# Running the second normalisation inside the last expert, with the short tile moved to the first unit

## The chip, the cores and the metric

One core of a Trainium2 chip runs the whole kernel. The metric is the device time in microseconds (us), median of three runs. Times in the text are us unless marked ns.

## The reference, cut to what matters

```
x = x + attention(x);  x = layernorm(x)            # (8, 1024, 256), no scale or bias
scores = softmax(x @ router_w.T)                   # 8 experts
gate, idx = top_k(scores per batch and expert, 257 tokens)
y = gelu(x[idx] @ w1 + b1) @ w2 + b2               # hidden width 1024
x = layernorm(x + scatter_add(y * gate at idx))    # the second normalisation
```

Each expert takes 257 tokens of each of the 8 batches. `layernorm` subtracts the mean of a row of 256 and divides by the square root of variance plus 1e-5.

## The kernel before, in words

The program is a row of stages: latent, attention, output projection with the first normalisation, the choice of tokens, the experts (`expert_stage`), and the second normalisation (`final_stage`). A stage is a block of its own: all engines meet at its end, and the next stage begins after that. Rows of `x` after the first normalisation stand in `x1_d` in HBM, with a second copy in `acc_d`, into which the experts add.

**Tiles and units (L1136 to L1141).** 257 tokens are two full tiles of 128 and one token left over. The left-over tokens of the 8 batches form one short tile of 8 rows. So an expert has 17 tiles: (batch 0, 0), (batch 0, 1), (batch 1, 0) and so on, and the short one last. `STARTS` cuts them into five units of 4, 4, 3, 3 and 3 tiles, with 512, 512, 384, 384 and 264 tokens.

**A unit on the engines.** GpSimd (POOL) gathers the token rows by an indirect DMA for each tile (L1258), two units ahead. TensorE (PE) transposes them (L1312), ScalarE (ACT) and VectorE (DVE) split them into a high and a low part. PE makes eight chunks of the hidden layer, each of six products (L1328 to L1330). ACT applies gelu (L1392), DVE splits the result (L1435, L1430). PE transposes the next unit's tokens, then makes the outputs of each tile with 24 products (L1343 to L1345). DVE adds the bias into `yb` (L1453), ACT multiplies by the gate into `yg` (L1381), and POOL adds the rows into `acc_d` by one indirect DMA a tile (`scatter`, L1262 to L1274), once the whole unit's `yg` is there. Buffers: four `raw` between gelu and split, four PSUM banks for hidden chunks, four output slots in PSUM, two each of `tok` and `yg`. Each engine runs its own list in program order. On ACT a unit is: eight gelus, split of the next tokens, gating (`gated`). On DVE: eight splits, low part of the next tokens, the bias adds. On POOL (`unit`, L1281): gather for two units ahead, a quarter of the next expert's weights (L1279, not in the last expert), scatter. So the eighth expert's ACT and DVE lists go on to the next unit only when the current unit's `yb` and `yg` are done.

**The end of the expert stage.** POOL waits for the landing of all scatters (L1294), SyncE (SP) has only loads of weights and biases to issue.

**The final stage (L1461 to L1549).** `acc_d` is cut into 16 groups of 512 rows, two to a batch, each held as 128 partitions of 4 rows. SP loads a group (four buffers). DVE measures it: four `bn_stats`, four `bn_aggr` (L1523, L1527). POOL turns the variance into the reciprocal root by two small instructions (L1504, L1506). DVE subtracts and scales in four passes (L1536) into a second buffer, and ACT's queue stores it to `out` (L1513).

Of the kernel before, what the change touches and what calls it, by code (L numbers as in the profile page):

```python
# [16 lines left out]
P = 128  # L17
# [1107 lines left out]
            sp.wait_ge(left_in, 32)  # L1125


def expert_stage(nc, w1, b1, w2, b2, W, x1_d, acc_d, idx_all, gate_all, idx_left, gate_left):

# [1 line left out]

    TILES = [(b, f, P) for b in range(B) for f in range(FULL)] + [(None, None, B)]  # L1136
    STARTS = [0, 4, 8, 11, 14, len(TILES)]
    UNITS = len(STARTS) - 1
    HC = HID // P
    YT = len(TILES)  # L1140
    HB = 4  # L1141
    RB = 4
    with ExitStack() as ctx:
        sb = lambda n, s, d=F32: ctx.enter_context(nc.sbuf_tensor(n, s, d))
        pb = lambda n, s, d=F32: ctx.enter_context(nc.psum_tensor(n, s, d))
# [13 lines left out]
        hid_lo = sb("hid_lo", [P, HC, HALF], F32R)  # L1159
        yb = sb("yb", [P, 4, C])  # L1160
        yg = [sb(f"yg{i}", [P, 4, C]) for i in range(2)]
        t_ps = [pb(f"e_t{i}", [P, HALF]) for i in range(2)]
        h_ps = [pb(f"e_h{i}", [P, HALF]) for i in range(HB)]
        y_ps = [pb(f"e_y{i}", [P, 2, C]) for i in range(2)]
# [1 line left out]
        b_in = [sem(f"b_in{u}") for u in range(2)]  # L1166
        tok_in = [sem(f"tok_in{i}") for i in range(2)]
        put = [sem(f"put{i}") for i in range(UNITS)]
        lists, turned, t_high, t_low, h_done, gelu_done, h_high, h_low, y_done, b_done, g_done = (
            sem(n) for n in ("lists", "turned", "t_high", "t_low", "h_done", "gelu_done", "h_high", "h_low",  # L1170
                             "y_done", "b_done", "g_done"))
# [5 lines left out]
        def tiles(g):  # L1177

            return [(q, *t) for q, t in enumerate(TILES[STARTS[g]:STARTS[g + 1]])]

        def batches(g):

            return {c for _, b, _, _ in tiles(g) for c in (range(B) if b is None else (b,))}

        def later(n, u, g, by, last):

# [9 lines left out]
        def landed(eng, g, n):  # L1196

            if not (isinstance(n, int) and n == 0):
                eng.wait_ge(put[g], 16 * len(tiles(g)) * n)
# [15 lines left out]
        def _(sp):  # L1215
# [19 lines left out]
            with sp.Fori(0, NE // 2 - 1) as i:  # L1235
                for u in range(2):
                    expert(2 * i + u, u)

        @block.gpsimd
        def _(pool):  # L1240
# [5 lines left out]
            pool.wait_ge(const_ready, 1)  # L1246
            pool.affine_select(out=ident[:], in_=ident[:], compare_op=ALU.not_equal, fill=1.0, base=0,
                               pattern=[[-1, P]], channel_multiplier=1).then_inc(const_ready, 1)

            def rows_of(u, b, f):  # L1250
                return idl[u][:, 0:1] if b is None else idx[u][:, f, b:b + 1]
# [29 lines left out]
            def unit(n, u, g, last):  # L1281

                ahead = later(n, u, g, 2, last)
                if ahead:
                    pool.wait_ge(turned, 2 * UNITS * n + 2 * g + 2)
                    gather(*ahead)
                if g < 4 and not (last and u == 1):
                    weights_low(n + 1, 1 - u, g)
                scatter(n, u, g)

            gather(0, 0, 0)
            gather(0, 0, 1)
            over_experts(pool, unit)
            for g in range(UNITS):  # L1294
                landed(pool, g, NE)

        @block.tensor
        def _(pe):
# [109 lines left out]
        def _(dve):  # L1408
# [15 lines left out]
            def unit(n, u, g, last):  # L1424
# [19 lines left out]
                if g == 2 and not (last and u == 1):  # L1444

                    for o in range(UNITS):
                        landed(dve, o, n)
                    make_lists(n + 1, 1 - u)
                for q, _, _, rows in tiles(g):
                    dve.wait_ge(y_done, YT * n + STARTS[g] + min(q // 2 * 2 + 2, len(tiles(g))))  # L1450

                    dve.wait_ge(g_done, YT * n + STARTS[g] + 1)
                    dve.tensor_tensor(yb[0:rows, q, :], y_ps[q // 2][0:rows, q % 2, :], b2s[u][0:rows, :],  # L1453
                                      ALU.add).then_inc(b_done, 1)

            make_lists(0, 0)
            tokens_low(0, 0, 0)
            over_experts(dve, unit)


def final_stage(nc, acc_d, out):  # L1461

    G = NTOK // HALF
    BUFS = 4
    with ExitStack() as ctx:  # L1465
        sb = lambda n, s, d=F32: ctx.enter_context(nc.sbuf_tensor(n, s, d))
        sem = lambda n: ctx.enter_context(nc.semaphore(n))
        expo = sb("f_expo", [P, 4])
        a = [sb(f"f_a{v}", [P, 4, C]) for v in range(BUFS)]
        o = [sb(f"f_o{v}", [P, 4, C]) for v in range(BUFS)]  # L1470
        stats = [sb(f"f_stats{v}", [P, 4, 6]) for v in range(2)]
        mv = [sb(f"f_mv{v}", [P, 4, 2]) for v in range(2)]
        rstd = [sb(f"f_rstd{v}", [P, 4]) for v in range(2)]
        a_in = [sem(f"f_a_in{v}") for v in range(BUFS)]
        o_out = [sem(f"f_o_out{v}") for v in range(BUFS)]
        passed = sem("f_passed")
        const_ready, stat_done, mv_done, var_done, rstd_done, o_done = (
            sem("f_" + n) for n in ("const", "stat_done", "mv_done", "var_done", "rstd_done", "o_done"))
        block = ctx.enter_context(nc.Block())
        rows = lambda d, i: d.rearrange("(g j p) c -> g p j c", p=P, j=4)[bass.ds(i, 1), :, :, :].rearrange(  # L1480
            "o p j c -> p (o j) c")

        @block.sync
        def _(sp):
            for v in range(BUFS):
                sp.dma_start(a[v][:], rows(acc_d, v)).then_inc(a_in[v], 16)
            with sp.Fori(1, G // BUFS) as i:
                for v in range(BUFS):

                    sp.wait_ge(o_done, BUFS * i + v - BUFS + 1)  # L1490
                    sp.dma_start(a[v][:], rows(acc_d, BUFS * i + v)).then_inc(a_in[v], 16)

        @block.gpsimd
        def _(pool):
            for v in range(BUFS):
                pool.sem_inc(o_out[v], 1)
            pool.memset(expo[:], -0.5).then_inc(const_ready, 1)
            pool.wait_ge(const_ready, 1)
            with pool.Fori(0, G // 2) as i:  # L1499
                for v in range(2):  # L1500
                    n = 2 * i + v
                    pool.wait_ge(mv_done, n + 1)
                    pool.sem_inc(passed, 1)  # L1503
                    pool.tensor_scalar(rstd[v][:], mv[v][:, :, 1], EPS, 1.0, ALU.add, ALU.mult).then_inc(var_done, 1)  # L1504
                    pool.wait_ge(var_done, n + 1)
                    pool.tensor_tensor(rstd[v][:], rstd[v][:], expo[:], ALU.pow).then_inc(rstd_done, 1)  # L1506

        @block.scalar
        def _(act):
            with act.Fori(0, G // BUFS) as i:  # L1510
                for v in range(BUFS):
                    act.wait_ge(o_done, BUFS * i + v + 1)
                    act.dma_start(rows(out, BUFS * i + v), o[v][:]).then_inc(o_out[v], 16)  # L1513
            for v in range(BUFS):
                act.wait_ge(o_out[v], 16 * (G // BUFS) + 1)

        @block.vector
        def _(dve):
            def measure(i, v):
                n = BUFS * i + v  # L1520
                dve.wait_ge(a_in[v], 16 * i + 16)
                for j in range(4):
                    dve.bn_stats(stats[v % 2][:, j, :], a[v][:, j, :]).then_inc(stat_done, 1)  # L1523
                for j in range(4):
                    dve.wait_ge(stat_done, 4 * n + j + 1)  # L1525
                    dve.sem_inc(passed, 1)  # L1526
                    ins = dve.bn_aggr(mv[v % 2][:, j, :], stats[v % 2][:, j, :])  # L1527
                ins.then_inc(mv_done, 1)

            def normalise(i, v):  # L1530
                n = BUFS * i + v
                dve.wait_ge(mv_done, n + 1)
                dve.wait_ge(rstd_done, n + 1)
                dve.wait_ge(o_out[v], 16 * i + 1)
                for j in range(4):
                    ins = dve.tensor_scalar(o[v][:, j, :], a[v][:, j, :], mv[v % 2][:, j, 0:1],  # L1536
                                            rstd[v % 2][:, j:j + 1], ALU.subtract, ALU.mult)
                ins.then_inc(o_done, 1)


            measure(0, 0)
            with dve.Fori(0, G // BUFS - 1) as i:  # L1542
                for v in range(BUFS):
                    measure(*((i, v + 1) if v < BUFS - 1 else (i + 1, 0)))
                    normalise(i, v)
            for v in range(BUFS):
                if v < BUFS - 1:
                    measure(G // BUFS - 1, v + 1)
                normalise(G // BUFS - 1, v)  # L1549


def post_ln_attention_moe(nc, x, x_t, w_down, w_k, w_v, w_q, w_out, router_t, w1, b1, w2, b2, out):
# [4 lines left out]
    with ExitStack() as ctx:  # L1557
# [9 lines left out]
        output_stage(nc, x, w_out, router_t, y_d, x1_d, acc_d, prob_all)  # L1567
        W = ExpertWeights(sb, sem)
        choose_stage(nc, w1, w2, W, prob_all, idx_all, gate_all, idx_left, gate_left)
        expert_stage(nc, w1, b1, w2, b2, W, x1_d, acc_d, idx_all, gate_all, idx_left, gate_left)  # L1570
        final_stage(nc, acc_d, out)


# [32 lines left out]
```

## Time and profile before

| | us |
|---|---|
| median of three runs | 3475.12 (3470.42 to 3476.35) |
| the profiled execution's own time | 3469.43 |
| its span, first to last instruction | 3467.5 |
| PE busy in the span | 3185.9 (92%) |
| DVE / ACT / POOL busy | 2097.3 / 1840.7 / 1388.5 |
| PE stage of the last expert | 3299.70 to about 3396.1 |
| first load of the final stage | 3411.20 |

Times in the rows below count from the span's start. Busy time is that of instructions; issue of DMAs on the SP and ACT queues doesn't count. PE's instructions overlap, so the distance between two starts says more than a duration.

### The profile page before, as it was taken

The page shows a single profiled execution, that of the slowest core. Times are in us where ns is not written, and L with a number is a line of the kernel's source. Part 1 is how long each engine was busy: PE and PEld are TensorE (multiplying, and loading weights), DVE is VectorE, ACT ScalarE, POOL GpSimd, SP SyncE. Part 2 cuts the span into 40 slices and gives each one's busy share as a digit, 9 for nine tenths or more (in the row PEclk, how much of TensorE's full clock was granted, in tenths as well). Part 3 has the DMA queues.
Part 4 walks back from the last instruction along what each step waited for, and adds up shares of the span by engine and source line. Part 5 has one row for each costly group of instructions (what it writes and reads, how often), then busy time and mean ns, then how long its engine had stood idle before and what let it go on. Part 6 is the DMA issues. An engine that isn't in the chain of part 4 may idle for free. (4 is left out here: it accounts for less than half of the span.)

```text
span 3467.5 us, 69523 instructions
## 1 busy us (share of the span) xinstructions
PE 3185.9 (92%) x21406; PEld 2506.0 (72%) x21406; DVE 2097.3 (60%) x4881; ACT 1840.7 (53%) x4007; POOL 1388.5 (40%) x1512
## 2 busy tenths in 40 slices
PE   5999999999999999999999999979908999999991
PEld 3767676667667676767676776679908999999991
DVE  1666566666666666666666666657584555455546
ACT  2667566666666666666666666633203343343430
POOL 0434343333334343334333333312214656565543
PEclk7999999999999999999999999989959999999996
DMA  6444444444445444444444444267402333333226
GB/s 204 106 114 108 99 113 104 102 102 119 104 100 123 101 107 110 108 98 114 107 99 117 106 111 101 65 250 268 180 27 64 72 68 74 67 76 68 41 42 202
DMA packets 184386, 376.26 MB, mean 109 GB/s; under 512 B 23872, under 2 KB 108224, under 8 KB 181952
## 3 DMA queue, kind: packets, MB, share of 16 engines
q1 hardware_dynamic: 144704, 308.52, 34.6%
q0 software_dynamic: 29696, 50.48, 7.3%
q10 hardware_dynamic: 9600, 12.58, 1.0%
q8 instruction: 184, 3.01, 0.4%
q14 instruction: 202, 1.65, 0.1%
HBM read 123.97 MB, written 79.76 MB: 59 GB/s over the span
## 5 line engine op out<-in xcount | busy, mean ns | idle before, releaser
L243 POOL TENSOR_SCALAR prob<-prob,inv 128x128 f32<-128x128 f32 (+7 forms) x1024 | 774.9, 757 | 1311.5 <-DVE inv L589 1311.5
L584 DVE TENSOR_REDUCE neg_max<-s_ps 128x1 f32<-128x128 f32 (+7 forms) x1024 | 773.2, 755 | 725.6 <-PE s_ps L370 709.9
L495 ACT ACTIVATE prob<-s_ps,neg_max 128x128 f32<-128x128 f32 (+7 forms) x1024 | 758.0, 741 | 199.6 <-DVE neg_max L584 182.4
L380 PE MATMUL t_ps<-ident,prob 128*128 128x128 f32 x4608 | 683.5, 275 | 9.1 <-ACT prob_t L573 2.5
L368 PE MATMUL s_ps<-k_hh,q_hl 128*128 128x512 f32 (+3 forms) x1536 | 591.6, 385 | 44.6 <-ACT prob L495 26.6
L573 ACT ACTIVATE prob_t<-t_ps 128x512 f32<-128x512 f32 (+3 forms) x768 | 415.8, 541 | 396.9 <-PE t_ps L380 396.2
L396 PE MATMUL o_ps<-prob_t,v 128*64 128x512 f32 (+3 forms) x3072 | 537.5, 492 | 1.5 <-DVE y L606 1.5
L369 PE MATMUL s_ps<-k_lz,q_hl 128*128 128x512 f32 (+3 forms) x1536 | 513.2, 346 | 0.0
L380 PEld LDWEIGHTS t_ps<-ident,prob 128*128 128x128 f32 x4608 | 495.7, 141 | 19.6 <-ACT prob_t L573 14.1
L368 PEld LDWEIGHTS s_ps<-k_hh,q_hl 128*128 128x128 f32 x1536 | 290.9, 189 | 176.4 <-issue 92.0
L396 PEld LDWEIGHTS o_ps<-prob_t,v 128*64 128x64 f32 x3072 | 203.8, 136 | 278.0 <-issue 251.6
L648 DVE COPY prob_t<-t_ps 128x128 f32<-128x128 f32 (+3 forms) x768 | 366.9, 478 | 57.1 <-PE t_ps L380 54.1
L369 PEld LDWEIGHTS s_ps<-k_lz,q_hl 128*128 128x128 f32 x1536 | 292.1, 190 | 32.1
L1343 PE MATMUL e_y<-w_hi,hid_hi 128*128 128x256 f32 (+1 forms) x1088 | 307.2, 282 | 0.0
L1345 PE MATMUL e_y<-w_hi,hid_lo 128*128 128x256 f32 (+1 forms) x1088 | 303.9, 279 | 0.0
L1344 PE MATMUL e_y<-w_lo,hid_hi 128*128 128x256 f32 (+1 forms) x1088 | 303.7, 279 | 0.0
L1271 POOL DMA_INDIRECT acc_d<-yg,idx x128 | 230.9, 1804 | 86.0 <-ACT yg L1381 52.4
L1392 ACT ACTIVATE raw<-e_h,b1s 128x512 f32<-128x512 f32 (+2 forms) x320 | 187.9, 602 | 138.4 <-PE e_h L1330 106.9
L1435 DVE CAST hid_hi<-raw 128x512 fp32r<-128x512 f32 (+2 forms) x320 | 172.6, 546 | 121.7 <-ACT raw L1392 120.8
L370 PE MATMUL s_ps<-mask_b,ident_b 128*128 128x128 bf16 x1024 | 236.2, 231 | 0.0
L1328 PE MATMUL e_h<-tok_hi,w_hi 128*128 128x384 f32 (+2 forms) x640 | 225.6, 352 | 4.4 <-issue 4.4
L1381 ACT ACTIVATE yg<-yb,gate 128x256 f32<-128x256 f32 x128 | 59.3, 503 | 320.2 <-DVE yb L1453 320.2
(152 smaller groups left out, 5502.7 us busy)
## 6 DMA issues: line engine op xcount, KB each, us to landing
k_hh<-k_high SPq DMA_DIRECT2D x256, 256.0 KB, 4.6
q_hl<-q_high SPq DMA_DIRECT2D x128, 256.0 KB, 4.0
q_hl<-q_low SPq DMA_DIRECT2D x128, 256.0 KB, 4.2
k_lz<-k_low SPq DMA_DIRECT2D x128, 256.0 KB, 5.4
y_d<-y SPq DMA_DIRECT2D x128, 256.0 KB, 3.8
c_yt<-y_d SPq DMA_DIRECT2D x16, 2048.0 KB, 8.5
w_raw<-w SPq DMA_DIRECT2D x16, 1024.0 KB, 7.5
a_xt<-x_t SPq DMA_DIRECT2D x8, 1024.0 KB, 7.6
```

What stands on the lines that cost most here:

```text
L243: pool.tensor_scalar(pr, pr, inv[:, s % 4:s % 4 + 1], 1.0, ALU.mult, ALU.mult).then_inc(norm_done, 1)
L368: pe.matmul(out, q_hl[u][h][:, cols], k_hh[u][h][:, w], start=True, stop=False)
L369: pe.matmul(out, q_hl[u][h][:, cols], k_lz[u][h][:, w], start=False, stop=True)
L380: mm = pe.transpose(t_ps[k % 2][:, j * P:(j + 1) * P], prob[s % 4][:, (first + j) * P:(first + j + 1) * P], ident[:])
L396: mm = pe.matmul(o_ps[64 * h:64 * h + 64, off:HALF], v[u][:, k, 64 * h:64 * h + 64], prob_t[g][:, h, k, off:HALF], start=(k == 0), stop=(k ...
L495: act.activation(prob[s % 4][:, 0:(q + 1) * P], s_ps[s % 2][:, 0:(q + 1) * P], ACT.Exp, bias=neg_max[:, s % 4:s % 4 + 1], accum_out=total[ ...
L573: act.activation(prob_t[g][:, h, b0:b0 + count, q % 4 * P:(q % 4 + 1) * P], t_ps[0][:, 0:count * P].rearrange("p (j c) -> p j c", c=P), AC ...
L584: dve.tensor_reduce(neg_max[:, s % 4:s % 4 + 1], s_ps[s % 2][:, 0:(q + 1) * P], AX.X, ALU.max, negate=True).then_inc(max_done, 1)
L648: dve.tensor_copy(prob_t[g][:, h, b0:b0 + count, q % 4 * P:(q % 4 + 1) * P], t_ps[1][:, 0:count * P].rearrange("p (j c) -> p j c", c=P)).t ...
L1343: pe.matmul(out, hid_hi[:, m, cols], W.w2_hi[u][:, w], start=(m == 0), stop=False)
L1344: pe.matmul(out, hid_hi[:, m, cols], W.w2_lo[u][:, w], start=False, stop=False)
L1345: mm = pe.matmul(out, hid_lo[:, m, cols], W.w2_hi[u][:, w], start=False, stop=(m == HC - 1))
```

## The change

`final_stage` is gone, and its work is in `expert_stage`. The short tile stands at place 3, and `STARTS` gives units of 4, 4, 4, 3 and 2 tiles (392, 512, 512, 384 and 256 tokens), in all eight experts. A batch ends with the unit that holds its second full tile: `ended(0)` is groups 0 and 1, `ended(1)` 2 to 5, `ended(2)` 6 to 9, `ended(3)` 10 to 13, `ended(4)` 14 and 15. In the last expert:

- SP waits for each unit's scatters to land and loads the groups that it ended into six buffers `fin`; group i needs the store of group i-6 landed.
- DVE measures the groups of the unit before: two ahead of its first bias add, two ahead of its third (in the unit of two tiles: behind its bias adds).
- POOL, after a unit's scatter, does for each group of the unit before the reciprocal root (`spread`) and, for groups 0 to 11, the four passes in place and the store from its own queue (`close`).
- DVE closes groups 12 to 15 behind everything, and SP stores them.

```
-    TILES = [(b, f, P) for b in range(B) for f in range(FULL)] + [(None, None, B)]
-    STARTS = [0, 4, 8, 11, 14, len(TILES)]
+    TILES = [(b, f, P) for b in range(B) for f in range(FULL)]
+    TILES.insert(3, (None, None, B))
+    STARTS = [0, 4, 8, 12, 15, len(TILES)]
+    G = NTOK // HALF;  FB = 6;  BY_POOL = G - 4
# SP, behind its loop over experts
+            for g in range(UNITS):
+                landed(sp, g, NE)
+                for i in ended(g):
+                    if i >= FB:
+                        sp.wait_ge(f_out[i % FB], 16 * (i // FB))
+                    sp.dma_start(fin[i % FB][:], rows_out(acc_d, i)).then_inc(f_in[i % FB], 16)
+            for i in range(BY_POOL, G):
+                sp.wait_ge(f_closed, i - BY_POOL + 1)
+                sp.dma_start(rows_out(out, i), fin[i % FB][:]).then_inc(f_last, 16)
# POOL
+            def spread(i):
+                pool.wait_ge(f_mv, i + 1)
+                pool.tensor_scalar(rstd[v][:], mv[v][:, :, 1], EPS, 1.0, ALU.add, ALU.mult).then_inc(f_var, 1)
+                pool.wait_ge(f_var, i + 1)
+                pool.tensor_tensor(rstd[v][:], rstd[v][:], expo[:], ALU.pow).then_inc(f_rstd, 1)
+            def close(i):
+                pool.wait_ge(f_rstd, i + 1)
+                for j in range(4):
+                    pool.tensor_scalar(fin[v][:, j, :], fin[v][:, j, :], mv[v][:, j, 0:1], rstd[v][:, j:j + 1],
+                                       ALU.subtract, ALU.mult).then_inc(f_scaled, 1)
+                pool.wait_ge(f_scaled, 4 * i + 4)
+                pool.dma_start(rows_out(out, i), fin[v][:]).then_inc(f_out[v], 16)
# POOL, unit()
                 scatter(n, u, g)
+                if last and u == 1 and g:
+                    for i in ended(g - 1):
+                        spread(i)
+                        if i < BY_POOL:
+                            close(i)
# DVE, unit()
+                closing = ended(g - 1) if last and u == 1 and g else []
+                for i in closing[:2]:
+                    measure(i)
                 for q, _, _, rows in tiles(g):
+                    if q == 2:
+                        for i in closing[2:]:
+                            measure(i)
                     (bias add of tile q)
+                if len(tiles(g)) <= 2:
+                    for i in closing[2:]:
+                        measure(i)
# at the end: POOL spread(14), spread(15); DVE close(12), close(13), measure(14), measure(15), close(14), close(15)
```

## Rows read from the trace of the kernel before

**Rows 1.** Windows: span; PE, PEld, DVE, ACT, POOL busy (count); granted clock; DMA.
```profile
3299.70:3396.20 96.50, 96.42 (x676) 90.52 (x674) 45.78 (x106) 35.05 (x65) 40.40 (x28) 1.00 0.25 38
...
3411.20:3467.50 56.30, 0.00 (x0) 0.00 (x0) 48.32 (x192) 0.00 (x0) 20.93 (x33) 0.50 0.89 298
```

**Rows 2.** Timeline of PE, last expert: start, duration, engine, line, operation.
```profile
3299.70 0.39 PE L1328 MATMUL e_h<-tok_hi,w_hi 128*128 128x512 f32 x1
...
3310.89 1.04 PE L1312 MATMUL e_t<-e_ident,tok 128*128 128x128 f32 x8
3311.68 0.36 PE L1343 MATMUL e_y<-w_hi,hid_hi 128*128 128x256 f32 x1
...
3323.08 0.40 PE L1328 MATMUL e_h<-tok_hi,w_hi 128*128 128x512 f32 x1
...
3372.14 1.05 PE L1312 MATMUL e_t<-e_ident,tok 128*128 128x128 f32 x6
3373.13 0.39 PE L1343 MATMUL e_y<-w_hi,hid_hi 128*128 128x256 f32 x1
```

**Rows 3.** Timeline of DVE and POOL, last expert: bias add, scatters.
```profile
3323.28 0.76 DVE L1453 TENSOR_TENSOR yb<-e_y,b2s 128x256 f32<-128x256 f32 x2 [4.84 <-PE e_y L1345]
...
3325.59 1.72 POOL L1271 DMA_INDIRECT acc_d<-yg,idx  x1 [13.24 <-ACT yg L1381]
...
3331.41 2.03 POOL L1271 DMA_INDIRECT acc_d<-yg,idx  x1 [0.30 <-issue]
...
3401.70 1.35 POOL L1271 DMA_INDIRECT acc_d<-yg,idl  x1 [0.30 <-issue]
```

**Rows 4.** Timeline of the final stage, its beginning and its last passes.
```profile
3411.20 2.22 SPq L1486 DMA_DIRECT2D f_a<-acc_d  x4
...
3415.07 1.41 DVE L1523 BATCH_NORM_STATS2 f_stats<-f_a 128x6 f32<-128x256 f32 x4 [18.49 <-DMA f_a<-acc_d]
3416.39 0.41 DVE L1527 BATCH_NORM_AGGREGATE f_mv<-f_stats 128x2 f32<-128x6 f32 x4
...
3418.60 1.38 DVE L1536 TENSOR_SCALAR f_o<-f_a,f_mv,f_rstd 128x256 f32<-128x256 f32 x4
3418.77 0.30 POOL L1504 TENSOR_SCALAR f_rstd<-f_mv 128x4 f32<-128x4 f32 x1 [0.43 <-DVE f_mv L1527]
3419.15 1.05 POOL L1506 TENSOR_TENSOR f_rstd<-f_rstd,f_expo 128x4 f32<-128x4 f32 x1
...
3462.54 1.39 DVE L1536 TENSOR_SCALAR f_o<-f_a,f_mv,f_rstd 128x256 f32<-128x256 f32 x4 [0.32 <-issue]
```

**Rows 5.** Groups by form, POOL: count | busy us, mean ns of one | idle.
```profile
L243 POOL TENSOR_SCALAR prob<-prob,inv 128x256 f32<-128x256 f32 x128 | 63.4, 496 | 189.2 <-DVE inv L589 189.2
...
L772 POOL DMA_DIRECT2D x_d<-c_x x16 | 12.9, 809 | 35.7 <-DVE c_x L897 35.7
```

**Rows 6.** DMA issues: queue, count, KB each, median us from issue to landing.
```profile
x_d<-c_x POOLq DMA_DIRECT2D x16, 512.0 KB, 4.5
...
f_a<-acc_d SPq DMA_DIRECT2D x16, 512.0 KB, 5.2
...
acc_d<-yg,idx POOLq DMA_INDIRECT x128, 3.9
```

**Rows 7.** Timeline of POOL and DVE, around the end of the seventh expert.
```profile
3286.84 2.40 POOL L1279 TENSOR_TENSOR w_lo<-w_raw,w_hi 128x1024 fp32r<-128x1024 f32 x1 [2.20 <-ACT w_hi L1365]
...
3291.39 3.64 POOL L1271 DMA_INDIRECT acc_d<-yg,idx  x1 [0.30 <-issue]
...
3301.24 1.01 POOL L1258 DMA_INDIRECT tok<-x_d,idx  x1 [0.30 <-issue]
```

**Rows 8.** Timeline of DVE in the same stretch.
```profile
3287.16 2.44 DVE L1435 CAST hid_hi<-raw 128x264 fp32r<-128x264 f32 x2 [1.89 <-ACT raw L1392]
...
3290.41 0.29 DVE L1435 CAST hid_hi<-raw 128x264 fp32r<-128x264 f32 x1
...
3290.96 0.28 DVE L1435 CAST hid_hi<-raw 128x264 fp32r<-128x264 f32 x1
```

More of the change, by code:

```diff
@@ L1125, in _, with expert_stage @@
             sp.wait_ge(left_in, 32)
-def expert_stage(nc, w1, b1, w2, b2, W, x1_d, acc_d, idx_all, gate_all, idx_left, gate_left):
-    TILES = [(b, f, P) for b in range(B) for f in range(FULL)] + [(None, None, B)]
-    STARTS = [0, 4, 8, 11, 14, len(TILES)]
+def expert_stage(nc, w1, b1, w2, b2, W, x1_d, acc_d, idx_all, gate_all, idx_left, gate_left, out):
+    TILES = [(b, f, P) for b in range(B) for f in range(FULL)]
+    TILES.insert(3, (None, None, B))
+    STARTS = [0, 4, 8, 12, 15, len(TILES)]
     UNITS = len(STARTS) - 1
@@ L1142, in expert_stage @@
     RB = 4
+    G = NTOK // HALF
+    FB = 6
+    BY_POOL = G - 4
     with ExitStack() as ctx:
@@ L1161, in expert_stage @@
         yg = [sb(f"yg{i}", [P, 4, C]) for i in range(2)]
+        expo = sb("f_expo", [P, 4])
+        fin = [sb(f"f_a{v}", [P, 4, C]) for v in range(FB)]
+        stats = [sb(f"f_stats{v}", [P, 4, 6]) for v in range(FB)]
+        mv = [sb(f"f_mv{v}", [P, 4, 2]) for v in range(FB)]
+        rstd = [sb(f"f_rstd{v}", [P, 4]) for v in range(FB)]
         t_ps = [pb(f"e_t{i}", [P, HALF]) for i in range(2)]
@@ L1168, in expert_stage @@
         put = [sem(f"put{i}") for i in range(UNITS)]
+        f_in = [sem(f"f_in{v}") for v in range(FB)]
+        f_out = [sem(f"f_out{v}") for v in range(FB)]
+        f_stat, f_mv, f_var, f_rstd, f_scaled, f_closed, f_last = (
+            sem(n) for n in ("f_stat", "f_mv", "f_var", "f_rstd", "f_scaled", "f_closed", "f_last"))
         lists, turned, t_high, t_low, h_done, gelu_done, h_high, h_low, y_done, b_done, g_done = (
@@ L1183, in batches, with ended @@
             return {c for _, b, _, _ in tiles(g) for c in (range(B) if b is None else (b,))}
+        def ended(g):
+            ends = {max(i for i, t in enumerate(TILES) if t[0] == b): b for b in range(B)}
+            return [2 * ends[i] + h for i in range(STARTS[g], STARTS[g + 1]) if i in ends for h in range(2)]
+        rows_out = lambda d, i: d.rearrange("(g j p) c -> g p j c", p=P, j=4)[i]
         def later(n, u, g, by, last):
@@ L1237, in _ @@
                     expert(2 * i + u, u)
+            for g in range(UNITS):
[7 more added lines that the diff above has]
+                sp.dma_start(rows_out(out, i), fin[i % FB][:]).then_inc(f_last, 16)
+            for v in range(FB):
+                sp.wait_ge(f_out[v], 16 * len(range(v, BY_POOL, FB)))
+            sp.wait_ge(f_last, 16 * (G - BY_POOL))
         @block.gpsimd
@@ L1248, in _ @@
                                pattern=[[-1, P]], channel_multiplier=1).then_inc(const_ready, 1)
+            pool.memset(expo[:], -0.5).then_inc(const_ready, 1)
+            pool.wait_ge(const_ready, 3)
+            def spread(i):
+                v = i % FB
+                pool.wait_ge(f_mv, i + 1)
+                pool.sem_inc(passed, 1)
+                pool.tensor_scalar(rstd[v][:], mv[v][:, :, 1], EPS, 1.0, ALU.add, ALU.mult).then_inc(f_var, 1)
+                pool.wait_ge(f_var, i + 1)
+                pool.tensor_tensor(rstd[v][:], rstd[v][:], expo[:], ALU.pow).then_inc(f_rstd, 1)
+            def close(i):
+                v = i % FB
+                pool.wait_ge(f_rstd, i + 1)
+                pool.sem_inc(passed, 1)
+                for j in range(4):
[3 more added lines that the diff above has]
+                pool.dma_start(rows_out(out, i), fin[v][:]).then_inc(f_out[v], 16)
             def rows_of(u, b, f):
@@ L1293, in _ @@
             over_experts(pool, unit)
-            for g in range(UNITS):
-                landed(pool, g, NE)
+            for i in ended(UNITS - 1):
+                spread(i)
         @block.tensor
@@ L1454, in unit, with measure, close @@
                                       ALU.add).then_inc(b_done, 1)
+                if len(tiles(g)) <= 2:
+                    for i in closing[2:]:
+                        measure(i)
+            def measure(i):
+                v = i % FB
+                dve.wait_ge(f_in[v], 16 * (i // FB) + 16)
+                for j in range(4):
+                    dve.bn_stats(stats[v][:, j, :], fin[v][:, j, :]).then_inc(f_stat, 1)
+                for j in range(4):
+                    dve.wait_ge(f_stat, 4 * i + j + 1)
+                    dve.sem_inc(passed, 1)
+                    ins = dve.bn_aggr(mv[v][:, j, :], stats[v][:, j, :])
+                ins.then_inc(f_mv, 1)
+            def close(i):
+                v = i % FB
+                dve.wait_ge(f_rstd, i + 1)
+                for j in range(4):
+                    ins = dve.tensor_scalar(fin[v][:, j, :], fin[v][:, j, :], mv[v][:, j, 0:1], rstd[v][:, j:j + 1],
+                                            ALU.subtract, ALU.mult)
+                ins.then_inc(f_closed, 1)
             make_lists(0, 0)
@@ L1458, in _ @@
             over_experts(dve, unit)
[L1461 to L1549, printed above, removed]
@@ L1552, in post_ln_attention_moe @@
+            for i in range(BY_POOL, ended(UNITS - 1)[0]):
+                close(i)
+            for i in ended(UNITS - 1):
+                measure(i)
+            for i in ended(UNITS - 1):
+                close(i)
 def post_ln_attention_moe(nc, x, x_t, w_down, w_k, w_v, w_q, w_out, router_t, w1, b1, w2, b2, out):
@@ L1569, in post_ln_attention_moe @@
         choose_stage(nc, w1, w2, W, prob_all, idx_all, gate_all, idx_left, gate_left)
-        expert_stage(nc, w1, b1, w2, b2, W, x1_d, acc_d, idx_all, gate_all, idx_left, gate_left)
-        final_stage(nc, acc_d, out)
+        expert_stage(nc, w1, b1, w2, b2, W, x1_d, acc_d, idx_all, gate_all, idx_left, gate_left, out)
 def kernel(**inputs):
```

## The prediction

> **What bounds the kernel now.** I read the windows first. In the last expert PE is busy for 96.42 of 96.50 us at full granted clock, POOL for 40.40 and DVE for 45.78 [rows 1]: PE sets the time, and DVE and POOL have room. In the final stage PE does nothing and DVE is busy for 48.32 of 56.30 us [rows 1]: DVE sets the time there, and POOL has 35 us free. Between them lies a hand-over: the last scatter is issued until 3403.05 [rows 3] and the first load starts at 3411.20 [rows 4]. From PE's end (3396.1) to the span's end (3467.5) are 71.4 us in which PE is idle. The change can only win there. The profiled execution's time is 3469.43, 1.9 over its span, and 5.7 under the median of the runs; I work out the difference in its span and put it on the median.
>
> **Units, all experts.** PE's starts give 11.19 for a hidden part of 512 tokens, 0.79 for the eight transposes behind it, 11.40 for the outputs of four tiles (2.85 a tile); where the short tile is among the transposed ones, 0.99 [rows 2]. By width, 392, 384 and 256 tokens take 8.57, 8.39 and 5.6. The widths sum to 2056 before and after and there are 17 tiles, so PE's work is the same; fewer transposes fall beside the slow short ones, which I estimate at -0.2 an expert. For seven experts that is -1, so the last one starts at 3298.7 instead of 3299.7. Times below count from there.
>
> Two gathers get closer to their use. POOL's fourth gather of the next expert's unit 1 starts at 3301.24 [rows 7]. No row shows a gather's landing; the scatter's 3.9 [rows 6] bounds it from above, and nothing excludes 1.0, its issue. By the bound it lands at 3305.1. Before, PE wants it at 3310.89 [rows 2]; now the last unit is 2.8 shorter and the first one's hidden part 2.6, so it wants it at 3305.5. The gather of unit 0 gains a tile of scatter (1.96) ahead of it and comes as close. Both fit, by 0.4 at worst. I cost them at nothing; if that cover goes, each us late costs 14 us (two places, seven experts).
>
> **The last expert, PE.** Units end at 20.8, 44.1, 67.3, 84.7 and, if nothing waits, 96.0.
>
> **Prices.** A scatter of four tiles takes 7.85 (3325.59 to 3333.44), so 1.96 a tile, and starts 1.55 behind the end of the last bias add [rows 3]. A scatter lands 3.9 after its issue, a POOL store 4.5 [rows 6]. A load takes 3.9 alone [rows 4] and 5.2 in the crowd [rows 6]; I take 3.9 for the first, 1.75 more for each next one of a burst (0.5 MB at 298 GB/s [rows 1]), and 4.6 for single ones. A measurement is 1.73, four DVE passes 1.4 [rows 4]. `spread` is 0.38 + 1.05 = 1.45 [rows 4]. A whole group on POOL: `spread` 1.45, four passes at 0.50, a store of 0.81 [rows 5], and some 0.45 for three hand-overs (0.08 between the two small instructions [rows 4], 0.30 behind a DMA [rows 3]): p = 4.7. Its passes have two column operands instead of one, which no row has on POOL. Below it could be 4.2 (hand-overs hidden, passes overlapping), above it 7.1 (every one of six POOL instructions waiting for a DVE instruction of 0.4). I take 4.7, since the nearest form ran 128 times at that mean.
>
> **The chain.** Scatter of unit 1 runs 46.4 to 54.3 and lands at 56.3; groups 2 to 5 load by 60.3, 62.0, 63.8, 65.5. DVE measures 2 and 3 until 63.8, adds two tiles, measures 4 and 5 until 69.0, adds the last two until 69.8, which is 2 later than unhindered. PE doesn't notice (four hidden banks). Behind the waiting DVE queue ACT's gating and gelus and DVE's splits. DVE then catches up without a pause. When it did so in the seventh expert (splits 0.55 apart [rows 8]), one indirect DMA took 3.64 instead of 1.6 [rows 7]; I add 2.1 for that. Unit 2's scatter: 71.3 to 81.3. POOL closes 2 to 5 until 81.3 + 4p = 100.1.
>
> Here is the new wait. Group 9 needs buffer 3, so group 3's store: issued at 81.3 + 2p - 1.1 = 89.6, landed 94.1, group 9 loaded 98.7, measured 100.4. Unit 3's third bias add stands behind it on DVE, ready since 84.7, and behind that ACT's gating, all gelus of unit 4 and DVE's splits. PE makes four hidden chunks of unit 4 and stands from about 88 to 101. That costs nothing by itself, because POOL's list is as late: scatter 3 can start at 102.3 and POOL is free at 100.1.
>
> From there POOL is the bound: scatter 3, 5.9 + 2.1 for the same catching up, until 110.3; groups 6 to 9, 4p = 18.8, until 129.1; scatter 4 (4.2 with its gap) until 133.3; groups 10 and 11 until 142.7; `spread` 12 and 13 until 145.6; DVE passes of 13 until 147.0; measurements of 14 and 15 until 150.5; `spread` 15, 1.5; passes of 15, 1.4: 153.4. In the final stage now the span ends 3.6 after the last pass (3463.93 to 3467.5 [rows 4]). So 157.0, and 3298.7 + 157.0 = 3455.7: **-12** on the span. PE's late unit 4 ends near 117 even at half clock (24 + 48 products at twice 0.118, the distance in 11.40/96), before DVE's measurements 10 and 11 let its bias add pass near 118; it is covered by POOL, which takes scatter 4 only at 129. The removed block boundary is in these numbers.
>
> **One rule against the row.** On the port: a cast of two took 2.44 while POOL ran the 2.40 weight split [rows 7, 8]; but `pow` took 1.05 beside DVE's passes and `bn_stats` [rows 4], as it did throughout. The Trainium skill ("SBUF — State Buffer", "Who interferes with whom") says that GpSimd and a DVE instruction in a two-port mode, `tensor_scalar` named among them, or with two SBUF inputs, lock each other out for the whole instruction. The first row agrees. The second doesn't: by the rule `spread` 13 would wait for DVE's passes of 12, +1.4, and the sum would be -10.6; by the row it is as above.
>
> **Rivals.**
> *POOL and DVE take turns* (slower). Each of six POOL instructions of a group waits for one DVE instruction of about 0.4: p = 7.1. With POOL the bound from 81.3 on, the end is 107.8 + 10p, that is 178.8, span 3477.5, +10. It decides from p = 6.1 (168.8, no gain) and makes it slower by over 0.2% from 6.8. For it: the 2.44 cast and the 3.64 scatter [rows 7, 8]. Against: `pow` [rows 4], and DVE mostly waits while POOL closes. Chance 0.10.
> *POOL's group is just dearer*, p from 5.4 to 6.8: between -7 and +7, say 6.1, no change. For it: the untried two-column form and the untested 0.45. Chance 0.14.
> *The gathers come late.* One us beyond the cover in both places gives -12 + 14 = +2. For it: a margin of 0.4 at the bound. Against: the bound is of a DMA that writes HBM. Chance 0.10, of which 0.03 slower.
> *More is won*: the 2.1 isn't paid (-4), p is 4.3 (-4): -20. Chance 0.13.
> *It doesn't overlap*, since DVE and POOL lists stall each other so far that PE's end matters: near -3. Chance 0.03.
>
> **How the numbers follow.** My forecast holds 0.50. Three runs tell about 0.2% (7 us) from nothing. Faster: 0.50 + 0.13 = 0.63. Same: 0.14 + 0.07 + 0.03 = 0.24. Slower: 0.10 + 0.03 = 0.13. 3475.1 - 12 = 3463. The likeliest case's own range is -16 to -8; the range goes from -22 (the faster rival with p = 4.2) to +2 (p = 6.3, or late gathers): 3453 to 3477.
>
> **What would show it.** An expert's period still about 97, with no PE wait on `tok`. In the last expert: DVE waiting for the load of group 9 ahead of the third bias add of unit 3; a gap of some 12 us in PE within unit 4's hidden part; POOL without a pause from scatter 3 to `spread` 13; POOL's passes near 0.5 and groups 4.7 apart; scatters beside DVE's catching up with one near 3.6. The forecast is wrong if POOL's groups are over 5.4 apart, if PE waits in the first seven experts, or if the end hangs on DVE or on stores instead of POOL.

## The result, and the profile after

The kernel after takes 3491.76 us, median of 5 runs (3489.72 to 3493.84), against 3474.03 of the kernel before beside it: ratio 1.0053, interval [1.0042, 1.0065]. It is slower by 17.7; the forecast was 12 faster, and the end of the range, 3477, was passed by 15. The profiled execution's span is 3490.0 (before 3467.5). Line numbers below are those of the kernel after: L1300 is POOL's pass, L1303 its store, L1326 the scatter, L1529 and L1533 DVE's measurement, L1540 DVE's pass.

The windows come first, as in [rows 1] and with the same columns: the last expert until the end that was forecast for PE if nothing waits, the stretch in which PE really ends, and the rest.

```profile
3305.79:3402.00 96.21, 87.66 (x604) 82.02 (x602) 53.10 (x152) 30.74 (x56) 65.33 (x53) 0.97 0.43 101
3402.00:3434.00 32.00, 10.20 (x72) 10.00 (x72) 11.59 (x45) 3.87 (x9) 27.79 (x27) 0.66 0.41 111
3434.00:3490.00 56.00, 0.00 (x0) 0.00 (x0) 13.47 (x55) 0.91 (x2) 42.65 (x44) 0.50 0.43 136
```

The fifth figure is POOL: 27.79 of 32, then 42.65 of 56. In the last stretch DVE, which was the bound in [rows 1], does 13.47, and DMA moves 136 GB/s instead of 298. So POOL holds the end. What it does all that time stands in its timeline (start, duration, engine, line, operation, wait ahead of it), here around groups 8 and 9:

```profile
3419.78 1.70 POOL L1326 DMA_INDIRECT acc_d<-yg,idx  x1 [0.31 <-issue]
...
3441.41 0.19 POOL L1291 TENSOR_SCALAR f_rstd<-f_mv 128x4 f32<-128x4 f32 x1
3441.68 1.03 POOL L1293 TENSOR_TENSOR f_rstd<-f_rstd,f_expo 128x4 f32<-128x4 f32 x1
3442.94 4.83 POOL L1300 TENSOR_SCALAR f_a<-f_a,f_mv,f_rstd 128x256 f32<-128x256 f32 x4 [0.22 <-POOL f_rstd L1293]
3448.07 0.85 POOL L1303 DMA_DIRECT2D out<-f_a  x1 [0.30 <-POOL f_a L1300]
3449.00 0.19 POOL L1291 TENSOR_SCALAR f_rstd<-f_mv 128x4 f32<-128x4 f32 x1
```

A group takes 3449.00 - 3441.41 = 7.59. The four passes are 4.83 of it, 1.21 each; all the rest is 2.76. The ten groups 2 to 11, on which the end hangs, take 78.2 together, 7.82 each: a few are longer, as told below. (The expectations below reckon with 7.65.) The prediction had 4.7: four passes at 0.50 from [rows 5], and 2.7 for the rest. The rest was right, the pass cost 2.4 times its estimate.

The waits that were forecast are there. DVE's queue, the load of group 9 and what stands behind it:

```profile
3402.31 1.41 DVE L1529 BATCH_NORM_STATS2 f_stats<-f_a 128x6 f32<-128x256 f32 x4 [3.73 <-DMA f_a<-acc_d]
3410.07 1.41 DVE L1529 BATCH_NORM_STATS2 f_stats<-f_a 128x6 f32<-128x256 f32 x4 [6.03 <-DMA f_a<-acc_d]
...
3477.55 2.84 DVE L1540 TENSOR_SCALAR f_a<-f_a,f_mv,f_rstd 128x256 f32<-128x256 f32 x8 [27.99 <-POOL f_rstd L1293]
...
3485.18 1.38 DVE L1540 TENSOR_SCALAR f_a<-f_a,f_mv,f_rstd 128x256 f32<-128x256 f32 x4 [0.25 <-POOL f_rstd L1293]
```

The measurement at 3410.07 is group 9's, ahead of unit 3's third bias add. ACT and PE stood behind it. The waits between 3380 and the end (waiting operation, releaser: us in all, times, longest):

```profile
ACT yg L1441 <- DVE yb L1519: 44.5, 3, 16.6
DVE f_stats L1529 <- DMA f_a<-acc_d: 42.7, 6, 11.9
DVE f_a L1540 <- POOL f_rstd L1293: 28.2, 2, 28.0
...
PE e_h L1388 <- ACT raw L1452: 19.0, 1, 19.0
```

PE stood 19.0 in unit 4's hidden part. The two long waits of DVE, 11.9 and 28.0, both end with something that POOL's list does late. A reader who ranks these waits by size would blame DVE's or PE's; whether POOL's list alone sets the end is tested below.

The seven experts before the last kept their 97.1 each, as forecast, but one pause grew. PE at the return of its loop over experts, before and then after:

```profile
3006.93 0.79 PE L1328 MATMUL e_h<-tok_hi,w_hi 128*128 128x512 f32 x1 [2.96 <-issue]
```

```profile
3011.95 0.69 PE L1388 MATMUL e_h<-tok_hi,w_hi 128*128 128x392 f32 x1 [5.22 <-issue]
```

### The profile page after: what moved, and what is told of

It reads as the page before. It is cut to its first block and busy times, and to the rows that moved or that the text cites. A ratio compares the mean times of both kernels' runs of the same rounds, so it can differ in the third digit from the quotient of the medians.

```text
span 3490.0 us, 69319 instructions
## 1 busy us (share of the span) xinstructions
PE 3192.1 (91%) x21406; PEld 2512.4 (72%) x21406; DVE 2082.4 (60%) x4833; ACT 1838.7 (53%) x4007; POOL 1439.8 (41%) x1572
## 5 line engine op out<-in xcount | busy, mean ns | idle before, releaser
L1452 ACT ACTIVATE raw<-e_h,b1s 128x512 f32<-128x512 f32 (+3 forms) x320 | 187.4, 602 | 138.5 <-PE e_h L1390 106.5
L1388 PE MATMUL e_h<-tok_hi,w_hi 128*128 128x512 f32 (+3 forms) x640 | 226.8, 354 | 25.4 <-ACT raw L1452 19.0
L1495 DVE CAST hid_hi<-raw 128x512 fp32r<-128x512 f32 (+3 forms) x320 | 174.2, 552 | 119.1 <-ACT raw L1452 118.4
L1326 POOL DMA_INDIRECT acc_d<-yg,idx x128 | 212.2, 1658 | 56.3 <-issue 34.9
```

## The experiments

The ratios are against the kernel before, run beside each. Where one starts from the kernel after, its diff is against that. S is the start of the last expert on PE; distances from S leave out what the stages ahead of it did.

**The price of each form on POOL.** The 12 groups that POOL closes go through three sets of instructions with the same buffers and waits, so each form runs four times. The kernel ran once, and its own time isn't used.

```
 # close(i); row(j), mean(j), inv(j) as in the change
+ i % 3 == 0: row,mean,inv subtract,mult | row,inv,1.0 mult,mult | row,mean,1.0 subtract,mult | row,0.5,1.0 subtract,mult
+ i % 3 == 1: row,mean,inv mult,mult | row,inv mult | 64 wide: subtract,mult | 128 wide: subtract,mult
+ i % 3 == 2: row,mean subtract | row,1.0,inv mult,mult | 512 wide: mean,inv subtract,mult
```

> The changed kernel, but GpSimd's passes on groups 0 to 11 take different forms, so that the normalised output is left out for these groups (a price list, its own time is not the point). In the changed kernel one pass of 256 with two column operands (mean and reciprocal root, subtract and multiply) took 1.21 us where I had 0.50. Theory A, the form: a second column operand is what costs; then forms with one column or none stay at 0.5, and two columns with multiply and multiply cost 1.2 too. Theory B, what runs beside it (VectorE, DMAs): all forms cost about 1.2 here. Theory C, the subtract or the in-place write: one column with subtract costs 1.2, two columns with multiply twice 0.5. The widths 64, 128, 256 and 512 with two columns tell whether the price goes by element (0.30, 0.60, 1.21, 2.4) or is a fixed addition of 0.7.

Measured, POOL's groups by form (count | busy us, mean ns | idle):

```profile
L1317 POOL TENSOR_SCALAR f_a<-f_a,f_mv,f_rstd 128x512 f32<-128x512 f32 x4 | 8.3, 2082 | 0.0
...
L1305 POOL TENSOR_SCALAR f_a<-f_a,f_mv 128x256 f32<-128x256 f32 x4 | 4.6, 1142 | 0.0
L1306 POOL TENSOR_SCALAR f_a<-f_a 128x256 f32<-128x256 f32 x4 | 4.3, 1072 | 0.0
L1309 POOL TENSOR_SCALAR f_a<-f_a,f_rstd 128x256 f32<-128x256 f32 x4 | 3.8, 940 | 0.0
...
L1310 POOL TENSOR_SCALAR f_a<-f_a,f_mv,f_rstd 128x64 f32<-128x64 f32 x4 | 2.4, 590 | 0.0
L1308 POOL TENSOR_SCALAR f_a<-f_a,f_mv,f_rstd 128x256 f32<-128x256 f32 x4 | 2.2, 553 | 0.9 <-POOL f_rstd L1293 0.9
```

The tile's name tells which operands are columns. L1308 has two and multiplies twice: 553. L1306 has none and subtracts: 1072. So the second column, which the prediction had named as the untried part, is cheap, and the subtraction is dear. L1310 and L1317 are the pass of the change at 64 and 512 wide: (2082 - 590) / 448 = 3.33 ns an element. L1309, one multiplication with no second operation, is dear too, and this run can't yet say whether it is "subtract" or "anything but two multiplications".

**Which operations.** The same frame, other forms: multiply-multiply by constants and at 64 wide, multiply-add and add-multiply with two columns, multiply-subtract, a copy, two-tensor operations.

```
+ i % 3 == 0: row,0.5,2.0 mult,mult | row,inv,mean mult,add | row,mean,inv add,mult | row,inv,mean mult,subtract
+ i % 3 == 1: row,mean,inv mult,mult | 64 wide: mean,inv mult,mult | row,mean,inv subtract,mult | row,mean,0.5 mult,add
+ i % 3 == 2: tensor_copy | tensor_tensor subtract | tensor_tensor mult
```

> A second price list in the changed kernel; GpSimd's passes take other forms, so the output of groups 0 to 11 is left out. The first list: 256 wide, multiply and multiply 0.48 (one column) to 0.55 (two columns), anything with a subtract 0.93 to 1.5, a single multiply without a second operation 0.94, subtract and multiply by width 0.59, 0.79, 2.08 for 64, 128, 512. Theory C (the operation pair decides): any pair other than multiply and multiply costs 1.0 to 1.2, multiply and add too; the constants 0.5 and 2.0 with multiply and multiply stay at 0.5. Theory D (only subtract is dear): multiply and add stays at 0.55, add and multiply too. A plain copy and tensor-tensor subtract and multiply of 256 are there for comparison (0.6 to 0.7 from the weight split, 1024 wide in 2.39).

```profile
L1306 POOL TENSOR_SCALAR f_a<-f_a,f_rstd,f_mv 128x256 f32<-128x256 f32 x4 | 4.9, 1237 | 0.0
L1310 POOL TENSOR_SCALAR f_a<-f_a,f_mv,f_rstd 128x256 f32<-128x256 f32 x4 | 4.9, 1226 | 0.0
...
L1314 POOL TENSOR_TENSOR f_a<-f_a 128x256 f32<-128x256 f32 x4 | 2.9, 720 | 0.0
L1315 POOL TENSOR_TENSOR f_a<-f_a 128x256 f32<-128x256 f32 x4 | 2.9, 720 | 0.0
L1305 POOL TENSOR_SCALAR f_a<-f_a,f_mv,f_rstd 128x256 f32<-128x256 f32 x4 | 2.3, 563 | 0.0
...
L1309 POOL TENSOR_SCALAR f_a<-f_a,f_mv,f_rstd 128x64 f32<-128x64 f32 x4 | 1.6, 388 | 0.0
```

Add-multiply (L1305) costs 563, multiply-subtract (L1306) 1237. So with two operations it is the subtraction that is dear, first or second, in this instruction; as a two-tensor operation it costs the 720 of a multiplication (L1314, L1315). The single multiplication (L1309 of the first list, 940) is a second dear form; why either is dear no run shows. Multiply-multiply grows by (552 - 388) / 192 = 0.85 ns an element, a quarter of the 3.33.

**Only the price taken away.** One column, multiply-multiply; everything else of the change stays.

```
-  pool.tensor_scalar(row, row, mean, inv, ALU.subtract, ALU.mult)
+  pool.tensor_scalar(row, row, inv, 1.0, ALU.mult, ALU.mult)
```

> The changed kernel, but GpSimd's passes on groups 0 to 11 only multiply by the reciprocal root, one column operand and a constant, as the attention stage does (the subtraction of the mean is left out). Theory A: a group on GpSimd falls from 7.65 to about 4.8 us, the end of the last expert's chain by 10 groups, some 27 us: about 3465 against 3492 of the changed kernel, 0.997 of the kernel before. Theory B (contention) or a theory by which another wait sets the end: no or little gain, 3485 to 3492.

```profile
3435.10 0.19 POOL L1291 TENSOR_SCALAR f_rstd<-f_mv 128x4 f32<-128x4 f32 x1
3435.37 1.04 POOL L1293 TENSOR_TENSOR f_rstd<-f_rstd,f_expo 128x4 f32<-128x4 f32 x1
3436.62 1.84 POOL L1300 TENSOR_SCALAR f_a<-f_a,f_rstd 128x256 f32<-128x256 f32 x4 [0.21 <-POOL f_rstd L1293]
...
3439.70 0.19 POOL L1291 TENSOR_SCALAR f_rstd<-f_mv 128x4 f32<-128x4 f32 x1
```

3457.0, ratio 0.9956 [0.9941, 0.9972]: about 16 faster than before and 35 faster than the kernel after. A group takes 4.60. I had expected 27 of gain. In the profiled executions the end comes 34.3 earlier behind S: the ten groups give some 31, scatter 2 ends 4.9 sooner because groups 0 and 1 are cheaper too, and 1.3 is lost as POOL now waits for data ahead of scatter 3. The last expert starts at 3303.60 and the span, 3453.5, ends at S + 149.9. The prediction's chain, step by step with 4.6 for p, gives 156.2, and 152.0 without its two catch-ups of 2.1, which are not seen (its short form 107.8 + 10p doesn't apply here, since it supposes that POOL never waits). So the chain holds to some 2 us, and the price alone turned its sign.

**The same result by a cheap form.** Two more small POOL instructions a group make the shift, minus mean times root, and the pass is multiply-add.

```
+  pool.tensor_scalar(neg, mean of 4 rows, -1.0, 1.0, ALU.mult, ALU.mult)
+  pool.tensor_tensor(neg, neg, rstd, ALU.mult)
-  pool.tensor_scalar(row, row, mean, inv, ALU.subtract, ALU.mult)
+  pool.tensor_scalar(row, row, inv, neg[:, j], ALU.mult, ALU.add)
```

> The changed kernel, whole output, but GpSimd's pass is x times reciprocal root plus (-mean times reciprocal root) instead of subtract and multiply; two more small instructions a group. Theory D: a pass of 0.55, a group of 5.3, so 23 us less than the changed kernel: about 3467. Theory C: passes stay at 1.2 or so, a group of 8.2: 3497.

```profile
3426.33 0.19 POOL L1292 TENSOR_SCALAR f_rstd<-f_mv 128x4 f32<-128x4 f32 x1
...
3428.49 2.16 POOL L1305 TENSOR_SCALAR f_a<-f_a,f_rstd,f_neg 128x256 f32<-128x256 f32 x4 [0.22 <-POOL f_neg L1301]
...
3431.85 0.19 POOL L1292 TENSOR_SCALAR f_rstd<-f_mv 128x4 f32<-128x4 f32 x1
```

3468.09, ratio 0.9981 [0.9972, 0.9991]. Four passes take 2.16 to 2.17, a group 5.52. S = 3308.33, span 3466.6, so S + 158.3; the chain, reckoned as in the last experiment and without the catch-ups, gives 159.4. That is 23.7 faster than the kernel after: the pair of operations in the pass, for two small instructions of 0.2 a group, decides between slower and faster.

**The units alone.** The kernel before with the short tile at place 3 and the new `STARTS`, its own `final_stage` kept.

```
+    TILES.insert(3, (None, None, B))
+    STARTS = [0, 4, 8, 12, 15, len(TILES)]
```

> The kernel before with only the new order of tiles and units (short tile at place 3, units of 4, 4, 4, 3 and 2 tiles); the final stage is a stage of its own as before. If the loss is all from GpSimd's closing: ratio to before 0.999 to 1.001 (+2 us at most, from the longer pause of TensorE where the loop over experts goes round: 5.2 against 3.0 us in the profiles). If the new units stall the experts: 1.002 or more.

3474.16, ratio 1.0002 [0.9993, 1.0011]: no difference. Its loop return takes 5.17, so that pause comes with the units and not with the moved stage. Late gathers would have shown here; none do.

**The buffers.** Ten `fin` instead of six, so that group 9 doesn't wait for the store of group 3.

```
-    FB = 6
+    FB = 10
```

> The changed kernel with ten group buffers instead of six, nothing else. Loads of groups 6 to 9 no longer wait for GpSimd's stores of 0 to 3, so VectorE's wait ahead of unit 3's third bias add and TensorE's stand of some 20 us inside unit 4 shrink to a few us. If GpSimd's list is the bound, the time hardly falls: 3488 to 3492. If the wait chain over the buffers (group 9 behind the store of group 3) were the bound, some 15 to 20 us fall: 3472 to 3477.

```profile
DVE f_a L1540 <- POOL f_rstd L1293: 39.2, 2, 38.9
...
PE e_h L1388 <- ACT raw L1452: 9.1, 1, 9.1
```

3494.26, ratio 1.0062 [1.0045, 1.0078]: the same as the kernel after. PE's stand is 10 shorter, though not down to the few us that I expected: DVE still waits for the loads of groups 6 and 7 (10.5), which need scatter 2 landed and not a buffer. DVE's wait for POOL is 11 longer. That is what a rearranged wait off the bound looks like, and it confirms that POOL's list, not the wait for buffers, sets the end.

**ScalarE closes the groups.** POOL keeps four small instructions a group; ACT does the passes in 0.50 each, DVE none. Groups 6 to 9 are closed only behind the last gating, and SP does all stores. Ten buffers.

```
+  pool: neg = -mean * rstd (as above); no passes, no stores
+  act.activation(row, row, Identity, bias=neg[:, j], scale=rstd[:, j])   # 4 a group
+  SP, behind the loads of unit g: stores (0,1) | (2,3) | (4,5) | (6,7,8) | 9 to 15
```

> The changed kernel with GpSimd's passes taken away for all 16 groups: ScalarE makes them (Identity with scale and bias columns, bias = -mean times reciprocal root, two more small GpSimd instructions a group), SyncE stores, ten buffers instead of six, groups 6 to 9 measured in the last unit instead of ahead of its gelus. If GpSimd's list was the bound, the end follows TensorE's: last scatter landed about 104 us after the last expert's start, two loads until 110, measurement, root, pass and store until 119: about 3427, 0.987 of before. Rival: ScalarE's gelus come late behind its passes or the passes cost over 0.7 each, then 3440 to 3455.

```profile
3309.10:3405.13 96.03, 96.03 (x676) 90.64 (x674) 58.56 (x169) 46.19 (x89) 54.26 (x59) 1.00 0.49 121
3405.13:3434.40 29.27, 0.00 (x1) 0.00 (x0) 14.07 (x66) 20.77 (x42) 17.46 (x37) 0.57 0.99 317
```

The chain that ended last has the last scatter's landing and the load behind it (start, duration):

```profile
3409.39 7.21 DMA acc_d<-yg,idx
3416.62 5.79 DMA f_a<-acc_d
```

3434.19, ratio 0.9887 [0.9872, 0.9902]: 39 faster than before. PE has no pause from S to S + 96.0. The end came at S + 125.3 instead of the 119 I expected, and the second window says why: no engine is busy for more than 20.77 of 29.27, but DMA is at 0.99 and 317 GB/s. Six loads and ten stores of 0.52 MB are 8.4 MB, 26.5 us at that rate. More than half of the miss is there in the chain: the last scatter lands 7.21 after its issue instead of 3.9 [rows 6], at S + 107.5 where I had 104. After PE's end the DMA is now most likely the bound; no run takes transfers away to show it.

**Two attempts to shorten that end.** First DVE closes 12 to 15, and the loads of 14 and 15 no longer stand behind the store of 8.

```
+    BY_DVE = G - 4          # DVE: measure 14, 15; then passes of 12 to 15
-    store (6, 7, 8) | 9 to 15
+    store (6, 7) | 8 to 15
```

> ScalarE's version (3434) with SyncE issuing the loads of groups 14 and 15 ahead of the store of group 8 (it held them up by 3 to 4 us), and VectorE making the passes of groups 12 to 15, which spares GpSimd two small instructions and ScalarE four passes for each. GpSimd's eight last roots then take 13.3 instead of 15.4, and the last pass ends some 5 us earlier: about 3429, 0.987. Rival: the order of landing decides and nothing changes, 3434.

```profile
acc_d<-yg,idx POOLq DMA_INDIRECT x2, 7.7
```

```profile
3419.16 1.41 DVE L1545 BATCH_NORM_STATS2 f_stats<-f_a 128x6 f32<-128x256 f32 x4 [4.44 <-DMA f_a<-acc_d]
...
3422.43 5.23 DVE L1556 TENSOR_SCALAR f_a<-f_a,f_mv,f_rstd 128x256 f32<-128x256 f32 x16
```

3434.18, ratio 0.9885 [0.9868, 0.9901]: nothing won. The two scatters of unit 4 (first row; median us to landing) share the DMA engines with loads and stores and land after 7.7 instead of 3.9 [rows 6], as late as in the version before (7.21); the loads behind them, and DVE's passes behind those, came late. I put it down to DVE's order and tried the other one:

```
-  measure(14); measure(15); finish(12); finish(13); finish(14); finish(15)
+  finish(12); finish(13); measure(14); measure(15); finish(14); finish(15)
```

> Edit: as in the previous version (groups 0 to 11 closed by ScalarE, 12 to 15 by VectorE), but VectorE closes groups 12 and 13 ahead of the measurements of 14 and 15 instead of behind them. My theory: in the previous version VectorE stood 4.44 us for the load of group 14 (until 3419.16) with the passes of 12 and 13 (8 passes, 2.6 us) still to do, and did them behind the measurements; in that gap they cost nothing, so the last pass and the end come 2.6 us earlier: about 3431.5, and about 1.5 us less if the stores of 12 and 13 also go out before the crowd. Rival: the end hangs on the stores in the queue (eight in a row, 12.6 us of issue), not on VectorE's list: then nothing is gained, 3434.

```profile
3408.53 1.56 POOL L1334 DMA_INDIRECT acc_d<-yg,idx  x1 [0.30 <-DVE f_mv L1549]
3416.08 0.93 SPq L1270 DMA_DIRECT2D f_a<-acc_d  x2
3417.05 11.57 SPq L1278 DMA_DIRECT2D out<-f_a  x8
...
3426.84 1.38 DVE L1556 TENSOR_SCALAR f_a<-f_a,f_mv,f_rstd 128x256 f32<-128x256 f32 x4 [0.26 <-POOL f_rstd L1308]
```

3433.6, ratio 0.9875 [0.9859, 0.9892], not told apart from the two before it. The last pass ends 119.7 behind S (3308.52) instead of 121.3, but the span ends 125.9 behind S in both. So the result is the rival's: the end doesn't hang on DVE's list. That it hangs on the transfers themselves fits the DMA share of 0.99 above, but isn't tested apart from SP's order of issue. Of the three versions none is better than the others within their intervals; all beat the kernel before by 1.1 to 1.3%.

## Why the prediction was wrong, point by point

**The step that failed** is in the prices: "four passes at 0.50", and with it p = 4.7. It took the price of a pass with one column and two multiplications for one with two columns, a subtraction and a multiplication. Measured: 1.21 a pass, 0.50 wrong by 0.71, times 40 passes = 28 us. Ten groups took 78.2 instead of 47, which makes 31.2 of the difference. The prediction's own list of signs had this one: it called itself wrong if groups were over 5.4 apart. The prediction doubted the right row for the wrong reason: it named the second column, worth 0.07 (553 against 481), and didn't look at the operation.

**The bounds failed with it.** The upper end of 7.1 came from DVE instructions getting in between, not from a dearer pass, so the measured 7.6 to 7.8 lay outside. Among the rows read, none of POOL had a subtraction of this kind; the nearest rows with other operations bound nothing. [rows 7] had a two-tensor subtraction on POOL at 2.40 for 1024 elements, 2.3 ns each. At that rate a pass would be 0.6 and p 5.1: it would not have warned either.

**The chain was right, to some 2 us.** With the measured p = 7.82 the prediction's formula for a late POOL gives an end at S + 107.8 + 78.2 = 186.0, and it came at 184.2 (3490.0 - 3305.79). The 1.8 between them is a balance. Scatter 3 took 2.3 less, scatter 4 0.3 less and the tail behind the groups 0.4 less, since the catch-ups cost the scatters nothing (1.5 to 1.8 each, none 3.64). Scatter 2 ended 1.2 later, at S + 82.5 instead of 81.3, because groups 0 and 1 had made POOL's list late already. With 7.59 for p, an undisturbed group, the formula gives 183.7, and that this is so near is luck, since two errors cancel. What lifts the mean from 7.59 to 7.82 is mostly this: group 5's passes took 5.50 instead of 4.83 while DVE caught up, and the stores of groups 6 and 10 were issued 1.15 and 0.76 behind their last pass instead of 0.31. With cheap passes the chain without the catch-ups is 2.1 off in one experiment and 1.1 in the other. The rest is balanced so: 3490.0 against 3455.7 is 34.3. Behind S stand 27.2 of it: 31.2 of the groups, less the 1.8, less 2.2 for which the forecast had POOL waiting ahead of scatter 3. Of the 7.1 ahead of S, 3.8 arose ahead of the expert stage, where both kernels are the same (it starts at 2601.4 instead of 2597.6). The seven experts took 2.3 more than before, all of it the loop return, where 1.0 less was forecast: the gain from the transposes isn't there.

**The new wait** was at its place, group 9 for the store of group 3, with PE's pause in unit 4: 19 long instead of 12, because p is larger. It cost nothing, as forecast; ten buffers took half of it away and won nothing.

**Each rival.** *POOL's group is just dearer* is what happened, beyond its own range of 5.4 to 6.8. *More is won* came true in its first half, the 2.1 that the scatters never paid, and was drowned by the price. *POOL and DVE take turns* had the right sign and threshold (slower by over 0.2% from p = 6.8) and not the mechanism of this loss: the pass costs 1.21 also at 3442.94, while DVE stands for a load. Smaller turns are there. Group 0's four passes took 6.05 instead of 4.84 and group 5's 5.50, each while DVE was splitting gelu results, and of the two only group 5 lies on the path. The lock that the prediction weighed (the Trainium skill, "SBUF — State Buffer", "Who interferes with whom") doesn't show where the prediction looked for it: `pow` beside DVE's passes of group 12 took 1.09 in the run with cheap passes, against 1.04 alone. No row says whether those DVE passes were in a two-port mode, so this pair is a weak test of that rule. The same rule, as the prediction gives it, holds for two inputs in SBUF as well, and `hid_lo` has them. In the first price list group 0's first pass fell beside two such instructions:

```profile
3360.54 2.42 POOL L1303 TENSOR_SCALAR f_a<-f_a,f_mv,f_rstd 128x256 f32<-128x256 f32 x1 [0.22 <-POOL f_rstd L1293]
3360.72 1.29 DVE L1507 TENSOR_TENSOR hid_lo<-raw,hid_hi 128x512 fp32r<-128x512 f32 x2
```

It took 2.42 instead of 1.22, longer by about what DVE's two took. This agrees with the Trainium skill, but group 5 lost only 0.7 beside eight such splits, and no run separates them. *The gathers come late*: PE waited for `tok` once, 0.7, in the last expert, and the units alone cost nothing. *It doesn't overlap*: in both versions with cheap passes POOL's list still sets the end, and PE's doesn't.

**A page on the failed step.** The Trainium skill ("GPSIMD Engine Reference", "Elementwise — side-by-side cycle accounting") gives 1.03 cycles an element for a body of at most two operations, at 1.2 GHz. The runs' 0.85 ns for multiply-multiply is 1.02 such cycles and agrees; the pass with a subtraction has two operations as well, and at 3.33 ns it is 4.0 cycles. Where the Trainium skill and these rows differ, the rows decide.

**The range and the chances.** The price was carried over two differences at once (columns and operation) into ten groups of the sum, and should have had a bound of its own. Even twice the known pass, 1.0, gives p = 6.7 and 3298.7 + 107.8 + 67 - 3467.5 = +6; the measured one is beyond that. The two rivals with a dearer group held 0.24 together, and the range ended at p = 6.3, inside them.

## What to carry to other kernels

Before work moves to another engine, price the very instruction there, operation for operation; a neighbour with the same shape and another operation isn't a bound, and on a path where it runs 40 times, half a microsecond is the sign of the change. When an estimate fails, put the measured price back into the old chain: if the chain then gives the measured end within a us or two, the price was what was wrong, and the cure is a cheaper form of the same step. And when the cure works, read the windows again, because the bound has moved: here from POOL to, as it seems, the DMA queues, where two more rearrangements of engines won nothing.

## What the runs showed of the hardware

- On POOL, `tensor_scalar` at 128x256 in f32 takes 0.45 to 0.56 with two multiplications or a multiplication and an addition, and 1.07 to 1.24 with a subtraction among the two, and 0.93 to 0.94 with one operation alone, be it a subtraction or a multiplication (single records that fell beside DVE's splits left out). The slopes with two operations are 0.85 and 3.33 ns an element. Why is open.
- A pass of POOL beside DVE's two-input `hid_lo` took 2.42 instead of 1.22 in one record, and four took 5.50 instead of 4.83; beside DVE's `tensor_scalar`, `pow` took 1.09 instead of 1.04.
- The same two-column subtract-multiply takes 0.35 a pass on DVE; multiply-and-shift on ACT takes 0.50.
- PE's pause at the return of the loop over experts went from 2.96 to between 5.1 and 5.6 in every kernel with the new units. What lengthens it was not tried.
- An indirect scatter lands in 3.8 to 3.9 in the kernels before and after, and in 7.2 to 7.7 beside loads and stores at some 300 GB/s.
